# Attention and feed-forward on one core: half chunk joined, table silu in four units, later rows turned by transfers, the triangle zeroed by GpSimd

## The chip, the cores and the metric

The kernel runs on one core of a Trainium2 chip. The core has TensorE (PE: matmul, with its own weight-load row PEld), VectorE (DVE), ScalarE (ACT), GpSimd (POOL), the queue of SyncE (SP), which here issues all transfers, and 16 DMA engines. The metric is the device time of one launch in microseconds (us), lower is better. The three timed runs of the kernel before gave 602.13 (median), 602.00 and 602.32 us.

## The reference

Four sequences (b) of 512 tokens with 256 features go through six residual sublayers:

```python
x = x + 0.5 * L0_ffn(layernorm(x))       # silu(gate) * up, int weights with per-row scales, 704 hidden
x = x + L0_attn(layernorm(x))            # 16 heads of 16, rope, causal softmax
x = x + 0.5 * L0_ffn(layernorm(x))
x = x + 0.5 * L1_ffn(layernorm(x))       # sigmoid(x1) * x2, ternary weights, 704 hidden
x = x + L1_attn(layernorm(x))            # 16 query heads on 4 key heads, alibi, causal softmax, bias
x = x + 0.5 * L1_ffn(layernorm(x))
```

All values are float32 in the reference. The kernel multiplies in float16 with each activation split into a high part and the rest (a low part), so most products are made twice.

## The kernel before

Each of the four sequences is one tile of 512 tokens as four blocks of 128 (`X[:, 4*b + t, :]`). There are 16 feed-forward units (`FFNS`, counted f) and 8 attention units (`ATT`, counted n, four of layer 0 and then four of layer 1). Nothing loops: each engine has a string in `ORDER` in which one letter is one step, and runs its steps strictly in that order. Steps of different engines meet through counting semaphores. Independent sequences are interleaved, so that TensorE always has a step of some unit. `banks` gives each TensorE step its bank of PSUM (8 banks of 128x512 float32).

A feed-forward unit: DVE statistics (`N`), POOL scale and offset (`r`, four small operations), ACT normalizes into `XN` (`X`, four activations), PE turns `XN` with eight 128x128 transposes against the identity (`t`, L498), ACT writes the high part `XT` (`x`, L703), DVE the low part (`t`, L871). The 704 hidden rows are five chunks of 128 and one of 64. PE makes gate (`g`) and up (`G`) of a chunk with four matmuls of 512 columns each (L520); for the chunk of 64 rows each of `g` and `G` is eight matmuls of 64x256, the two halves of the tokens put into the two halves of the output partitions (L517). ACT takes tanh of half the gate (`t`, L719 for layer 0, L721 for layer 1). In layer 0, DVE makes silu from it in a step of its own (`s`, L885) and multiplies with up (`h`, L895); in layer 1 one DVE step does it (L898). ACT writes the high part `HH[0]` (`h`, L728), POOL the low part `HH[1]` (`h`, L1018). The buffer `TH` for these has three slots. The down product is `z` (eight matmuls for the half chunk, L537) and four `d` of ten matmuls (L549).

An attention unit: `e`/`Y`/`u`/`y` do the same normalizing and turning (L1012, L696, L498, L709, L876), `q` and `v` project (L565, L581), layer 0 is rotated by rope (`p`, `q` on DVE, `s`, `a` on POOL, through the buffers `QF` and `QS`), and SP's transfers `k` stack heads into `SQ` and `SK`. Each unit then has four groups Q of four heads. For a group PE makes the scores with queries as rows in five steps (`m`, L599) for the row maxima (`MX`, DVE L940 and L944), turns the maxima (`x`), SP inserts them as one more row of `SQ` (`r`, a transfer), and PE makes the scores again with keys as rows, maximum already subtracted, in five steps (`s`, L621). Every `m` and every `s` step ends with four mask matmuls (L470) that add -1e30 above the diagonal. ACT takes the exponential of two banks at a time into `PB` (`e`, L764, 128x1024), and PE multiplies with V (`p`, L639), which waits for the group's five exponentials only. ACT copies the result (`o`, L774). The softmax denominators go through SP (`D`, `S`, `R`: `DC`, a scratch in HBM, and back broadcast as `RB`), POOL divides (`c`, L1050) and splits (`C`, L1054), PE projects (`o`, L654) and DVE adds to `X` (L957).

## Time and profile of the kernel before

| | us |
|---|---|
| median of three timed runs | 602.13 |
| the profiled execution, its own time | 603.93 |
| its span in the trace | 601.9 |
| PE busy | 552.0 |
| DVE busy | 448.0 |
| ACT busy | 393.6 |
| POOL busy | 285.8 |

The trace shows the profiled execution. Busy time of PE is modelled with the tail of each pipelined matmul, so a row of consecutive matmuls costs less than its count times its mean; the start of the next group says what it cost. Each wait in the trace names what released it.

### The profile page before, as it was taken

The numbers are of one execution on the slowest core, as the hardware profiler recorded it, in microseconds if no ns is written. First come the engines' busy times: TensorE is split into PE (matmuls) and PEld (weight loads), VectorE is DVE, ScalarE is ACT, GpSimd is POOL, SyncE is SP. The second block draws the span as 40 slices with busy tenths as digits, with TensorE's granted clock in tenths as the row PEclk, the third lists the DMA queues.
The fourth block names the chain that finished last, engine by engine and source line by source line (L and its number), as shares of the span: only waits on it lengthen the run. The fifth ranks groups of instructions, "written<-read, shape, count | busy, mean of one in ns | idle before, by whom it ended". The sixth has DMA issues, their size and how long they took to land.

```text
span 601.9 us, 14116 instructions
## 1 busy us (share of the span) xinstructions
PE 552.0 (92%) x5772; PEld 317.3 (53%) x5772; DVE 448.0 (74%) x778; ACT 393.6 (65%) x628; POOL 285.8 (47%) x311
## 2 busy tenths in 40 slices
PE   2898888988899999999999999999999999899996
PEld 1455444455554756465654564656555556554554
DVE  4799998986788749985798786876777787773343
ACT  5776443674587666867487758478577676779442
POOL 5596989532477275842613345352333331025433
PEclk9999989998999999999999999999999999999999
DMA  8600010020121000211011011000200112010100
GB/s 337 282 2 2 35 71 25 31 79 15 38 75 71 21 19 2 89 60 43 1 67 41 30 32 53 23 17 29 78 21 20 38 67 75 21 41 18 73 36 35
DMA packets 17183, 31.82 MB, mean 53 GB/s; under 512 B 4656, under 2 KB 6064, under 8 KB 16968
## 3 DMA queue, kind: packets, MB, share of 16 engines
q1 hardware_dynamic: 17120, 30.93, 13.9%
q8 instruction: 45, 0.74, 0.5%
q14 instruction: 18, 0.15, 0.1%
HBM read 13.75 MB, written 2.36 MB: 27 GB/s over the span
## 4 chain that ended last, share of the span: by engine, by line
PE 46%; DMA 14%; DVE 12%; ACT 10%; POOL 8%; issue 6%; SPq 2%; POOLq 0%; DVEq 0%; ACTq 0%
PE PS L520 14%; PE PS L639 8%; DMA RB<-scratch 7%; PE PS L549 7%; ACT PB L764 5%; DMA scratch<-DC 3%; PE PS L565 3%; DVE MX L944 3%; PE PS L599 3%; PE PS L621 3%; PE PS L654 3%; DMA DC<-OT 2%; POOL OC L1050 2%; PE PS L470 2%; DVE XT L871 2%
## 5 line engine op out<-in xcount | busy, mean ns | idle before, releaser
L764 ACT ACTIVATE PB<-PS 128x1024 f32<-128x1024 f32 x160 | 156.4, 1028 | 42.0 <-PE PS L470 41.4
L944 DVE TENSOR_REDUCE MX<-PS 128x2 f32<-128x1024 f32 (+2 forms) x192 | 157.1, 863 | 19.5 <-PE PS L470 18.9
L520 PE MATMUL PS<-XT,WGU 128*128 128x512 f16 x640 | 151.1, 384 | 3.9 <-ACT TH L721 1.3
L1018 POOL TENSOR_TENSOR HH<-TH,HH 128x512 f16<-128x512 f32 (+1 forms) x96 | 104.2, 1101 | 85.7 <-ACT HH L728 85.6
L520 PEld LDWEIGHTS PS<-XT,WGU 128*128 128x128 f16 x640 | 58.8, 99 | 73.9 <-issue 4.6
L470 PE MATMUL PS<-MASKM,MASKW 64*128 64x128 bf16 (+1 forms) x1280 | 82.1, 206 | 0.0
L728 ACT ACTIVATE HH<-TH 128x512 f16<-128x512 f32 (+1 forms) x96 | 56.2, 595 | 32.6 <-PE PS L549 14.0
L549 PE MATMUL PS<-WD,HH 128*128 128x256 f16 x640 | 76.0, 274 | 1.0 <-POOL HH L1018 1.0
L639 PE MATMUL PS<-PB,V 128*32 128x512 f32 (+3 forms) x1024 | 75.5, 436 | 0.7 <-ACT PB L764 0.5
L470 PEld LDWEIGHTS PS<-MASKM,MASKW 64*128 64x128 bf16 x1280 | 57.7, 95 | 25.6 <-issue 0.8
L549 PEld LDWEIGHTS PS<-WD,HH 128*128 128x128 f16 x640 | 60.9, 98 | 11.8 <-POOL HH L1018 1.5
L599 PE MATMUL PS<-SK,SQ 63*128 63x256 f16 (+3 forms) x512 | 59.9, 302 | 6.8 <-DVE MX L944 2.9
L621 PE MATMUL PS<-SQ,SK 64*128 64x384 f16 (+3 forms) x512 | 58.8, 303 | 7.0 <-ACT PB L764 2.9
L898 DVE SCALAR_TENSOR_TENSOR TH<-TH,PS 128x512 f32<-128x512 f32 (+1 forms) x48 | 30.4, 642 | 42.5 <-PE PS L520 20.5
L1050 POOL TENSOR_TENSOR OC<-OC,RB 128x512 f32<-128x512 f32 x16 | 20.3, 1272 | 78.6 <-DMA RB<-scratch 78.6
L639 PEld LDWEIGHTS PS<-PB,V 128*32 128x32 f32 x1024 | 30.1, 110 | 41.8 <-issue 32.0
L565 PE MATMUL PS<-XT,WA 128*128 128x512 f16 (+1 forms) x168 | 42.7, 397 | 2.8 <-ACT OT L774 1.4
L498 PE MATMUL PS<-ID,XN 128*128 128x128 f32 x192 | 29.3, 288 | 14.5 <-ACT XN L689 11.2
L940 DVE TENSOR_REDUCE MX<-PS 128x4 f32<-128x1024 f32 x32 | 38.9, 1216 | 2.9 <-PE PS L470 2.9
L689 ACT ACTIVATE XN<-X,OFF,YR 128x256 f32<-128x256 f32 x64 | 33.1, 593 | 11.7 <-POOL OFF L1000 11.7
L788 DVE BATCH_NORM_STATS2 ST<-X 128x6 f32<-128x256 f32 x96 | 33.7, 412 | 6.7 <-DMA X<-x_in 5.9
L719 ACT ACTIVATE TH<-PS,SGH 128x512 f32<-128x512 f32 (+1 forms) x48 | 30.3, 648 | 10.3 <-POOL HH L1018 8.2
(99 smaller groups left out, 726.4 us busy)
## 6 DMA issues: line engine op xcount, KB each, us to landing
SQ<-QPB SPq DMA_DIRECT2D x24, 256.0 KB, 2.4
OC<-OT SPq DMA_DIRECT2D x16, 256.0 KB, 2.4
RB<-scratch SPq DMA_DIRECT2D x32, 128.0 KB
SK<-QPB SPq DMA_DIRECT2D x12, 256.0 KB, 2.3
out<-X SPq DMA_DIRECT2D x4, 512.0 KB, 3.3
PB<-wd SPq DMA_DIRECT2D x2, 768.0 KB, 8.9
PB<-gu SPq DMA_DIRECT2D x2, 704.0 KB, 5.9
X<-x_in SPq DMA_DIRECT2D x2, 512.0 KB, 5.2
```

What stands on the lines that cost most here:

```text
L470: m = e.matmul(to, MASKW[64 * z:64 * z + 64, way, half, :], by, start=False, stop=True, skip_group_check=True)
L520: m = e.matmul(o[:, :], WGU[l][:, k, col:col + P], XT[0][j][:, k, :], start=first, stop=last)
L549: m = e.matmul(o[:, z, q * D:(q + 1) * D], HH[j][:, s * T + t * P:s * T + (t + 1) * P], WD[l][:, s, :], start=False, stop=s == FC - 2 and ...
L565: m = e.matmul(o[0:width, :], WA[l][:, jw, k, ch * P:ch * P + width], XT[1][jx][:, k, :], start=s == 0 and k == 0, stop=s == 2 and k == 1)
L599: e.matmul(o[:, z, col:col + kw], SQ[n % 2][64 * z:64 * z + QROWS - 1, 2 * g + pr, t * P:(t + 1) * P], SK[n % 2][64 * z:64 * z + QROWS - 1 ...
L621: e.matmul(o[:, z, col:col + T - kb * P], SK[n % 2][64 * z:64 * z + QROWS, 2 * g + pr if l == 0 else pr, kb * P:(kb + 1) * P], SQ[n % 2][6 ...
L639: m = e.matmul(o[32 * a:32 * a + 32, kb * P:T], V[:, kb, 4 * g + a if l == 0 else a, :], PB[i % 2][:, s, a % 2, col:col + T - kb * P], sta ...
L728: e.activation(HH[0][:, s * T:s * T + wd], TH[:, i % 3, 0:wd], ACT.Copy).then_inc(f_hi, 1)
L764: e.activation(PB[Q % 2][:, j, :, :], two_banks("s", i), ACT.Exp, scale=0.25).then_inc(a_exp, 1)
L940: e.tensor_reduce(MX[:, Q % 4, :, :, 1], o.rearrange("p a (r k) -> p a r k", r=2), AX.X, ALU.max, negate=True).then_inc(a_max, 1)
L944: e.tensor_reduce(MX[:, Q % 4, :, pr, t], o[:, :, col:col + (t + 1) * P], AX.X, ALU.max, negate=True).then_inc(a_max, 1)
L1018: e.tensor_tensor(HH[1][:, s * T:s * T + wd], TH[:, i % 3, 0:wd], HH[0][:, s * T:s * T + wd], ALU.subtract).then_inc(f_lo, 1)
```

## The change

Five things change, and all order strings and bank numbers are written anew.

1. Half chunk joined. The weight columns are laid out so that the 64 gate columns and the 64 up columns of the half chunk lie side by side. One `g` of four 512-column matmuls makes both (gate in partitions 0 to 63, up in 64 to 127); `G` exists for five chunks only. ACT and DVE now work on 64x512 for this chunk where they worked on 128x256. Its low part is made by DVE (`k`, a new step) and not by POOL, into partitions 64 to 127 of `HH[0]`, so that one matmul per token block does high and low of it in the down product: `z` is gone and `d` has eleven matmuls. `d` takes one bank for two token blocks.
2. Table silu. In the first four units (`SILU = 4`) ACT applies Silu itself, and the DVE step `s` is dropped there. Exponentials wait until the last of these has run.
3. Rows turned by transfers. From feed-forward unit 6 on (`TF`) and for the four layer-1 attention units (`TA`), ACT writes the high half of `XN` and DVE the low half as float16 into buffers that lie over `QF` and `QS`, 128x1024 each, and SP issues one transposing transfer for each half (`T`, `U`). PE's transposes of these units are dropped.
4. Exponentials above the diagonal zeroed on POOL. The mask matmuls after `s` are dropped, except in group 0 of each layer-1 unit. In the 28 other groups POOL's new step `f` sets the upper triangle of each diagonal block of `PB` to zero, and `p` waits for it.
5. Orders and banks anew.

```diff
+SILU = 4
+TF, TA = 6, NB
+CUTS = [(1, [(0, T, 4), (2 * T + 384, T, 2)]), (3, [(4 * T, T, 4), (6 * T + 384, T, 2)]), (4, [(8 * T, 256, 4)])]
+CUTQ = [Q for Q in range(4 * NA) if ATT[Q // 4][1] == 0 or Q % 4 > 0]
 # orders: the first line of PE, before and after
-        "ttGgggggGGGgGGagzttGGgggddddGgggGGGzttggddddguuagGGqqvvGggGGqGztqtuugggGqqGdGddmdGmgmmmmxgqmmssmsmsqx"
+        "ttgGggGGGaggGgttGGddggGddggagGgGtutuddddqvgggGqGGvggqGgGqttuuddddGqqgggggmmGgqmGGmGmmqxmmmssmsmxmssm"
 # SP
+                elif c == "T":
+                    k, j = divmod(i, 2)
+                    f = TF + k
+                    w.wait_ge(f_gate, FC * f)
+                    w.wait_ge(f_up, (FC - 1) * f)
+                    w.wait_ge(f_half[j], k + 1)
+                    e.dma_start_transpose(XT[0][j][:, :, :, :].rearrange("p t k q -> p (t k) q"),
+                                          XHF[j].rearrange("p t d -> p (t d)")).then_inc(f_dma[j], 16)
...
 # PE, gate and up
-                            if s == FC - 1:
-                                for z in range(2):
-                                    m = e.matmul(o[64 * z:64 * z + 64, 0:256], WGU[l][:, k, col:col + 64],
-                                                 XT[0][j][:, k, 256 * z:256 * z + 256], start=first, stop=last)
-                            else:
-                                m = e.matmul(o[:, :], WGU[l][:, k, col:col + P], XT[0][j][:, k, :],
-                                             start=first, stop=last)
+                            m = e.matmul(o[:, :], WGU[l][:, k, col:col + P], XT[0][j][:, :, k, :],
+                                         start=j == 0 and k == 0, stop=j == 1 and k == 1)
...
 # PE, scores with keys as rows
-                    m = mask(o, 1, [col for pr, kb, col in SSTEP[j]])
+                    if l == 1 and g == 0:
+                        m = mask(o, 1, [col for pr, kb, col in SSTEP[j]])
 # PE, product with V
+                    w.wait_ge(a_tri, NTRI * sum(Q <= i for Q in CUTQ))
 # ACT
+                    if f < SILU:
+                        e.activation(TH[0:rows, i % 3, :], src, ACT.Silu, scale=SG1[0:rows, s:s + 1]).then_inc(f_tanh, 1)
+                    e.activation(XHF[0], XN[0][:, :, :], ACT.Copy).then_inc(f_half[0], 1)
 # DVE
+                    e.tensor_tensor(XHF[1], XN[0][:, :, :], XHF[0], ALU.subtract).then_inc(f_half[1], 1)
+                    e.tensor_tensor(HH[0][64:P, (FC - 1) * T:FC * T], TH[0:64, FC * i % 3, :], hi,
+                                    ALU.subtract).then_inc(f_lh, 1)
 # POOL
+                elif c == "f":
+                    j, Q = i % NTRI, CUTQ[i // NTRI]
+                    st, cuts = CUTS[j]
+                    w.wait_ge(a_exp, NS_T * Q + st + 1)
+                    for c0, d, nb in cuts:
+                        blk = PB[Q % 2][:, :, :, :].rearrange("p s z (b n) -> p (s z b) n", n=P)[:, c0 // P:c0 // P + (nb - 1) * d // P + 1:d // P, :]
+                        m = e.affine_select(blk, blk, [[0, nb], [1, P]], ALU.is_ge, 0.0, base=0, channel_multiplier=-1)
+                    m.then_inc(a_tri, 1)
```

Three places show how the orders moved. TensorE in the middle of the attention work, before: every score step is followed by its masks (L621 with L470 behind it).

```order
L621 MATMUL PS<-SQ,SK 128x512 x2
L470 MATMUL PS<-MASKM,MASKW 128x64 x4
L621 MATMUL PS<-SQ,SK 128x384 x2
L621 MATMUL PS<-SQ,SK 128x128 x2
L470 MATMUL PS<-MASKM,MASKW 128x2x64 x4
L565 MATMUL PS<-XT,WA 128x512 x6
```

And after, where `s` is L674, `m` is L652 and the masks are L538:

```order
L674 MATMUL PS<-SQ,SK 128x384 x2
L674 MATMUL PS<-SQ,SK 128x128 x2
L674 MATMUL PS<-SQ,SK 128x512 x2
L674 MATMUL PS<-SQ,SK 128x384 x2
L674 MATMUL PS<-SQ,SK 128x128 x2
L694 MATMUL PS<-PB,V 32x512 x4
L694 MATMUL PS<-PB,V 32x384 x4
L694 MATMUL PS<-PB,V 32x256 x4
L694 MATMUL PS<-PB,V 32x128 x4
```

Score steps of the second kind now follow each other with nothing between them; the masks stay behind the first kind.

GpSimd around a middle attention unit, before (L1018 low part of the hidden values, L991 to L1000 and L1006 to L1012 scale and offset, L1030 to L1038 rope, L1050 and L1054 the attention output):

```order
L1018 TENSOR_TENSOR HH<-TH,HH 128x256
L1034 TENSOR_TENSOR QF<-QF,QS 128x512
L1018 TENSOR_TENSOR HH<-TH,HH 128x512
L1054 TENSOR_TENSOR CH<-OC,CH 128x512
L1038 TENSOR_TENSOR QPB<-QF,QPB 128x512
L1018 TENSOR_TENSOR HH<-TH,HH 128x512 x4
L991 TENSOR_SCALAR VE<-MV 128x4
```

And after (L1149 the selects, L1121 the low part, L1110 to L1116 scale and offset, L1162 the division):

```order
L1149 AFFINE_SELECT PB<-PB 128x4x128
L1121 TENSOR_TENSOR HH<-TH,HH 128x512 x3
L1149 AFFINE_SELECT PB<-PB 128x4x128
L1149 AFFINE_SELECT PB<-PB 128x2x128
L1162 TENSOR_TENSOR OC<-OC,RB 128x512
L1149 AFFINE_SELECT PB<-PB 128x4x128
L1149 AFFINE_SELECT PB<-PB 128x2x128
L1110 TENSOR_SCALAR VE<-MV 128x4
L1111 TENSOR_SCALAR OFF<-MV 128x4
L1113 TENSOR_TENSOR YR<-VE,HALF 128x4
L1116 TENSOR_TENSOR OFF<-OFF,YR 128x4
L1149 AFFINE_SELECT PB<-PB 128x4x128
```

The selects stand between the division, the scale and offset of the next unit and the low parts, five to a group.

SyncE's queue in layer 1, before (L424 the maxima row, L431 and L435 out of `OT`, L441 and L450 to and from the scratch):

```order
L431 DMA DC<-OT 64x1x64
L435 DMA OC<-OT 128x1x512
L424 DMA SQ<-NM 2x8x128
L441 DMA scratch<-DC 64x64
L450 DMA RB<-scratch 64x1x512 x2
L424 DMA SQ<-NM 2x8x128 x2
```

And after (L499, L503, L474, L509, L518 for the same, L483 and L492 the new transfers for feed-forward and attention):

```order
L483 DMA_TRANSPOSE XT<-QF 128x8x128 x2
L499 DMA DC<-OT 64x1x64
L503 DMA OC<-OT 128x1x512
L474 DMA SQ<-NM 2x8x128
L509 DMA scratch<-DC 64x64
L483 DMA_TRANSPOSE XT<-QF 128x8x128 x2
L474 DMA SQ<-NM 2x8x128
L518 DMA RB<-scratch 64x1x512 x2
```

The transposing transfers stand ahead of the denominators' way out, and between its way out and its way back.

## Rows read from the trace of the kernel before

**Rows 1.** The page, part 1: busy time, share of span, instructions.
```profile
PE 552.0 (92%) x5772; PEld 317.3 (53%) x5772; DVE 448.0 (74%) x778; ACT 393.6 (65%) x628; POOL 285.8 (47%) x311
```

**Rows 2.** Windows of five stretches: length, then busy us (instructions) of each engine, clock, DMA.
```profile
15.00:92.00 77.00, 68.75 (x430) 38.39 (x429) 71.30 (x135) 46.77 (x83) 59.37 (x59) 0.98 0.19 77
...
110.00:330.00 220.00, 208.31 (x2360) 120.66 (x2355) 174.16 (x302) 151.30 (x237) 107.99 (x115) 0.99 0.12 43
330.00:550.00 220.00, 212.71 (x2500) 122.26 (x2494) 160.78 (x263) 155.78 (x246) 75.11 (x85) 1.00 0.11 39
550.00:602.00 52.00, 45.03 (x349) 27.32 (x348) 19.23 (x35) 23.48 (x42) 21.16 (x22) 0.99 0.11 42
```

**Rows 3.** The page, part 4: the chain that ended last, by engine.
```profile
PE 46%; DMA 14%; DVE 12%; ACT 10%; POOL 8%; issue 6%; SPq 2%; POOLq 0%; DVEq 0%; ACTq 0%
```

**Rows 4.** Timeline of PE at 373 us: start, us, group.
```profile
373.36 0.61 PE L537 MATMUL PS<-WD,HH 64*128 64x256 f16 x8
373.81 0.38 PE L621 MATMUL PS<-SQ,SK 64*128 64x256 f16 x4
374.03 0.28 PE L470 MATMUL PS<-MASKM,MASKW 64*128 64x128 bf16 x4
374.14 0.38 PE L599 MATMUL PS<-SK,SQ 63*128 63x512 f16 x2
374.36 0.22 PE L470 MATMUL PS<-MASKM,MASKW 64*128 64x64 bf16 x4
374.42 0.38 PE L599 MATMUL PS<-SK,SQ 63*128 63x384 f16 x4
...
376.52 4.54 PE L549 MATMUL PS<-WD,HH 128*128 128x256 f16 x40
380.90 1.04 PE L498 MATMUL PS<-ID,XN 128*128 128x128 f32 x8
381.87 0.64 PE L639 MATMUL PS<-PB,V 128*32 128x512 f32 x4
```

**Rows 5.** Timeline at 33 us, PE's rows of the half chunk.
```profile
33.70 0.63 PE L517 MATMUL PS<-XT,WGU 128*64 128x256 f16 x8
...
34.26 1.90 PE L520 MATMUL PS<-XT,WGU 128*128 128x512 f16 x8
...
36.00 4.53 PE L549 MATMUL PS<-WD,HH 128*128 128x256 f16 x40
```

**Rows 6.** Groups by shape: busy us, mean ns of one, idle before and its releaser.
```profile
L885 DVE SCALAR_TENSOR_TENSOR TH<-TH,PS 128x512 f32<-128x512 f32 x40 | 26.7, 681 | 6.0 <-ACT TH L719 5.8
L898 DVE SCALAR_TENSOR_TENSOR TH<-TH,PS 128x256 f32<-128x256 f32 x8 | 3.3, 416 | 4.3 <-PE PS L517 1.9 <-ACT TH L721 1.3 <-PE PS L520 1.1
L764 ACT ACTIVATE PB<-PS 128x1024 f32<-128x1024 f32 x160 | 156.4, 1028 | 42.0 <-PE PS L470 41.4
L790 DVE TENSOR_REDUCE FM<-X 128x64 f32<-128x1024 f32 x8 | 9.6, 1202 | 0.0
L1018 POOL TENSOR_TENSOR HH<-TH,HH 128x512 f16<-128x512 f32 x80 | 93.6, 1187 | 47.6 <-ACT HH L728 47.5
L1018 POOL TENSOR_TENSOR HH<-TH,HH 128x256 f16<-128x256 f32 x16 | 10.7, 671 | 38.1 <-ACT HH L728 38.1
L974 POOL MEMSET SK<- 128x1024 f32 x4 | 3.7, 952 | 0.0
L667 ACT ACT_TABLE_LOAD x1 | 1.3, 1283 | 0.7 <-PEq L1179 0.7
```

**Rows 7.** The page, part 6: the stacking transfers: count, size, us to landing.
```profile
SQ<-QPB SPq DMA_DIRECT2D x24, 256.0 KB, 2.4
```

**Rows 8.** Timeline of the tail, all engines.
```profile
574.03 4.54 PE L549 MATMUL PS<-WD,HH 128*128 128x256 f16 x40
577.85 2.07 ACT L689 ACTIVATE XN<-X,OFF,YR 128x256 f32<-128x256 f32 x4 [4.83 <-POOL OFF L1000]
582.99 8.81 PE L520 MATMUL PS<-XT,WGU 128*128 128x512 f16 x40
```

293 lines of the change are left out of this document (181 added, 112 removed).

## The prediction

> **What bounds the kernel now.** I read the page's busy times first [rows 1]. The reader sees TensorE at 552.0 of 601.9 us, so its idle time is 49.9 us; the next engine, DVE, has 448.0. Then the stretches [rows 2]. In the attention work from 110 to 550 us PE is busy 208.3 + 212.7 = 421.0 of 440 us, 96%, while DVE has 335.0, ACT 307.1 and POOL 183.1. There only less PE work or dearer waiting moves the time. From 15 to 92 us (the first feed-forward units and the preparation of the weights) the picture is another one: DVE is busy 71.3 of 77 us, PE 68.8. The chain that ended last gives PE 46%, DMA 14%, DVE 12%, ACT 10%, POOL 8% [rows 3]: 8% and 14% are what the path already spends on the two resources that this change loads. Last, the timelines for what a group of matmuls really costs, from its start to the next group's start, since a single one's mean holds the tail of the pipeline.
>
> **Masks after `s`.** A two-block mask starts at 374.03 and the next group at 374.14: 0.11 us. A one-block mask is 374.36 to 374.42: 0.06 us [rows 4]. A group of heads has three of the first and two of the second, 0.45 us. Dropped in 28 of 32 groups: 12.6 us of PE.
>
> **Transposes.** Eight take from 380.90 to 381.87, 0.97 us [rows 4]. Ten feed-forward and four attention units lose theirs: 14 x 0.97 = 13.6 us of PE.
>
> **Half chunk.** Eight matmuls of L517 start at 33.70, the next group at 34.26: 0.56 us, some of it the switch to the wide form [rows 5]. The two steps `g` and `G` cost 1.12. Eight wide matmuls take 34.26 to 36.00, so 0.2175 each [rows 5], and the joined step costs 0.87. Saved: 0.25 x 16 = 4.0 us. It is no more because the two 64-column halves already run side by side (eight of 256 columns in 0.56 us). In the down product `z` took 373.36 to 373.81, 0.45 us, and the four matmuls that replace it cost 4 x 4.38 / 40 = 0.44 (from 376.52 to 380.90) [rows 4]: nothing. PE together: 12.6 + 13.6 + 4.0 = 30.2 us, leaving 521.8.
>
> **DVE.** Table silu drops 24 steps, 20 of 681 ns and 4 of about 416: 15.3 us, all before the attention work [rows 6]. The half chunk widens 20 remaining DVE steps (16 products, 4 silu) from 256 to 512 columns, 681 - 416 = 265 ns each: +5.3. The new step `k` is a 512-column subtraction, taken at 681 too: 16 x 0.681 = +10.9. The low halves of the turned rows were 28 steps of the same width (19.1 us) and become 14 of 1024 columns, for which the nearest rows give 1.20 (one input) and 2 x 0.681 = 1.36 us: +16.8 to +19.1. I take the latter, the same kind of operation. DVE ends up 0.9 us higher over all, but 15.3 - 6 x (0.265 + 0.681) = 9.6 us lower in the first stretch. There PE, with 8.3 us idle and six units' half chunks less (1.5 us), becomes the bound quickly. I take 5 us for the shortened idle, between 0 (the waits are then on POOL or the weights) and 8.3.
>
> **ACT.** Fourteen 1024-column activations at 1.03 (the exponential's row) replace 28 of half the width; 32 half-chunk steps widen, at DVE's 265 ns about 8.5 us. ACT has 307 of 440 us in the attention work and absorbs it. The change of function adds two table loads of 1.28 us [rows 6], 2.6 us. The order puts the first before the first Silu and the second before the first exponential. Both can lie in a wait for PE; I charge 1.3, bounds 0 and 2.6.
> The Trainium skill's page "ScalarE: Activation LUTs" (What ACT_TABLE_LOAD costs) gives 1,283 ns for the load, as the row does, and about 1,380 ns of drain with it. By it two switches would cost 5.3 us, 2.7 more than by the row; no row here shows the drain.
>
> **POOL.** It loses 16 low parts of 671 ns, 10.7 us. It gains 28 groups x (three selects of 512 columns and two of 256). The trace has no select. Below stands the memset, 952 ns for 1024 columns, hence 0.48 and 0.24: 1.9 us a group, 53 us. Above stand the two-input subtractions of 1187 and 671 ns [rows 6]: 4.9 us a group, 137 us. A select reads once and writes once, between the two; I take the middle, 3.4 us a group, 95 us. POOL comes to 285.8 - 10.7 + 95 = 370, not the bound. But it works in order: a select that waits for its exponential holds up the low parts behind it (`HH`, hence the `TH` slot and the down product), and the division of the attention output. And `p` now waits for the last select, 0.5 to 1.2 us after the last exponential.
>
> **Transfers.** 28 new ones of 256 KB. A stacking transfer of that size lands after 2.4 us [rows 7]. Before, the last row of `XT` was ready 582.99 - 579.92 = 3.1 us after `XN` was finished [rows 8]. Now: 1.03 for the high half, about 1.3 for the low, 2.4 for its landing: 4.7, so 1.6 us later. In 13 of 14 places other units' work covers this on PE. In the tail PE was idle from 578.57 to 582.99 except for the transposes. The new order leaves 20 wide matmuls (4.4 us) beside the 44 of the down product (4.8) for this stretch, 9.2 us instead of 4.8, so the tail is covered as well: 0, and 3 us if that cover fails.
> The Trainium skill's page "Advanced Engine Details and Errata" (X-Bar Transpose) says that transposing transfers run as fast as regular ones, but its section on software and hardware descriptor generation calls the hardware queue the worse one for transposes. The first agrees with my use of the stacking row; the second, which has no figure, speaks against this change. No row here shows either.
>
> **What the attention work gives back.** PE's demand there falls from 421 by 12.6, by 12.6 of the transposes (one tail unit apart) and by about 2.5 of the half chunks, to 393 us. The others stay: DVE 335 + 6, POOL 183 - 7 + 95 = 271. At today's 96% that would take 411 us; DVE would then be at 83%, where it was 76%. With less slack on DVE and the select in every group's path I expect PE at 93.5%: 420 us, 9 to 10 us given back. Bounds: 0, and the whole 28.
>
> **The sum**, on the span: 601.9 - 30.2 - 5.0 + 1.3 + 10.0 = 578.0. The timed median stands 0.2 us above the span, and so I forecast 578.
>
> **Rivals.**
> A, everything is gained: selects near the memset's price, and the attention work stays at 96%. Then 578 - 10 - 3 = 565. For it: PE's waits now are short and spread. Against: one more engine in every group.
> B, POOL takes PE's place in the path: selects at the subtraction's price. POOL in the attention work is then 183 - 7 + 137 = 313 of 412 us, the `p` steps wait 0.4 to 0.8 us in each of 28 groups and the low parts behind them: 12 us more given back, 590. For it: POOL's 8% of the chain. Against: POOL was idle for 257 of 440 us.
> C, slower: a transposing transfer holds the SP queue. The 28 stand in that queue ahead of the maxima row and of the denominators' way out and back, which the chain already holds with 14%. With a hold of h us each, all on the path, the 24 us of gain are gone at h = 0.86; at 2 us it is 578 + 56 - 24 of slack that the maxima row has = 610. For it: nothing in the trace shows how such a transfer is issued. Against: a plain one of this size has landed after 2.4 us [rows 7], so its own hold is shorter, and most of the 28 would have to stand on the path.
> That the change doesn't do what it says: the instructions are plainly gone from PE, so this has no share of its own.
>
> **Chances.** Forecast (568 to 586) 0.55; A 0.12; B (586 to 601) 0.13; C above 603.3 0.15; and 0.05 for an end within 0.2% of 602.13, which is about what a measurement of this kernel can tell from no change. Faster by more: 0.80. The range leaves out C (0.15) and the lower third of A (0.05): 562 to 602.
>
> **What would show each step.** PE's busy time near 522 and 560 fewer masks; first exponential about 5 us earlier and DVE under 90% in the first stretch; a select of 512 columns between 0.5 and 1.2 us, and `p` released by POOL for under 0.5 us in the mean; transposing transfers landing near 2.4 us with SP never blocked by them; PE above 93% of the attention work. What would make me wrong: selects above 1.2 us, transfers above 4 us, or new orders whose waits have nothing to do with these five steps.

## The result, and the profile after

The changed kernel takes 611.58 us (median of 4 runs, 610.09 to 612.43), the kernel before beside it 602.07. The ratio is 1.0156, 95% interval 1.0135 to 1.0177: slower by 9.5 us, where the forecast was 578 and the range ended at 602. The profiled execution's span is 610.0 us against 601.9.

First the page after, its busy times (they answer to [rows 1]), TensorE's granted clock in 40 slices, and the chain that ended last ([rows 3]):

```profile
PE 531.2 (87%) x4844; PEld 285.7 (47%) x4844; DVE 456.0 (75%) x758; ACT 401.0 (66%) x616; POOL 354.2 (58%) x435
PEclk9988999799979999999999999799999999999999
PE 33%; DVE 16%; POOL 15%; ACT 15%; DMA 10%; issue 9%; SPq 2%; POOLq 0%; DVEq 0%; ACTq 0%
```

PE has lost 20.8 us of busy time where my sum took 30.2 away, and its idle time rose from 49.9 to 610.0 - 531.2 = 78.8 us. The mean granted clock fell from 0.991 to 0.972: in six stretches, 34.0 us together, PE ran at 1.2 instead of 2.4 GHz, and it was busy for 29.0 us of them. PE's share of the chain fell from 46% to 33%, and POOL's rose from 8% to 15%.

The same three stretches as in [rows 2], after (length, busy us of PE, PEld, DVE, ACT, POOL, clock, DMA share, GB/s):

```profile
15.00:92.00 77.00, 66.11 (x375) 38.93 (x373) 61.00 (x116) 47.67 (x83) 60.77 (x61) 0.93 0.20 78
110.00:330.00 220.00, 198.08 (x1956) 106.14 (x1953) 172.30 (x276) 152.08 (x227) 137.23 (x178) 0.96 0.19 54
330.00:550.00 220.00, 202.11 (x2095) 106.17 (x2091) 175.42 (x275) 157.55 (x239) 109.76 (x141) 0.98 0.23 56
```

DVE in the first stretch is where I expected it (71.30 - 9.6 = 61.7, here 61.00), and PE there has not become faster. In the attention work PE is busy 91% of the time, where I took 93.5%.

The groups that are new after, with the mean ns of one, how long `p` waits for a select (idle us, times; the matmuls' row PE and the weight loads' row PEld, whose waits can lie side by side), and the transposing transfers with their us to landing:

```profile
L1149 POOL TENSOR_SCALAR_AFFINE_SELECT PB<-PB 128x512 f32<-128x512 f32 x84 | 55.6, 662 | 58.9 <-ACT PB L841 58.7
L1149 POOL TENSOR_SCALAR_AFFINE_SELECT PB<-PB 128x256 f32<-128x256 f32 x56 | 22.8, 407 | 0.0
L1001 DVE TENSOR_TENSOR HH<-TH,HH 64x512 f16<-64x512 f32 x16 | 15.1, 942 | 1.0 <-ACT HH L804 0.6
L952 DVE TENSOR_TENSOR QF<-XN,QF 128x1024 f16<-128x1024 f32 x10 | 16.1, 1607 | 4.3 <-ACT QF L763 4.2
L957 DVE TENSOR_TENSOR QS<-XN,QS 128x1024 f16<-128x1024 f32 x4 | 4.9, 1221 | 1.6 <-ACT QS L769 1.5
...
  PE PS L694: 6.4, 6
  PEld PS L694: 2.9, 2
...
XT<-QF SPq DMA_TRANSPOSE x20, 3.2
XT<-QS SPq DMA_TRANSPOSE x8, 3.3
```

To see where the time went, three marks are read from each trace: the start of the first `p`, the start of the last group's `p`, and the span's end. Kernels built for the experiments are in the table too; the ratio is to the kernel before, timed beside each.

| kernel | ratio, 95% interval | first `p` at | from there to the last group's `p` | from there to the end |
|---|---|---|---|---|
| before | 1 | 114.8 | 438.6 | 48.5 |
| after | 1.0156 (1.0135 to 1.0177) | 122.4 | 434.0 | 53.6 |
| a_nosel | 1.0019 (0.9984 to 1.0054) | 120.5 | 426.0 | 53.0 |
| a_masks | 1.0025 (0.9998 to 1.0053) | 120.2 | 426.0 | 53.5 |
| a_selfew | 1.0011 (0.9976 to 1.0046) | 121.8 | 428.0 | 52.1 |
| a_seltiny | 1.0060 (1.0016 to 1.0104) | 121.7 | 425.5 | 53.7 |
| a_selmove | 1.0133 (1.0083 to 1.0182) | 121.5 | 433.1 | 53.2 |
| a_plain | 1.0147 (1.0096 to 1.0198) | 121.8 | 436.0 | 53.4 |
| a_silu0 | 1.0424 (1.0372 to 1.0476) | 137.9 | 436.0 | 53.7 |
| m_tail | 1.0015 (0.9980 to 1.0051) | 121.5 | 428.3 | 54.2 |
| m_noturn | 1.0281 (1.0216 to 1.0345) | 120.7 | 439.0 | 57.3 |
| b_nomask | 0.9869 (0.9826 to 0.9913) | 112.4 | 430.7 | 48.0 |
| b_sel | 1.0256 (1.0186 to 1.0326) | 113.4 | 454.4 | 49.5 |
| b_selfew | 0.9999 (0.9966 to 1.0033) | 115.1 | 438.0 | 48.4 |
| b_silu | 1.0058 (1.0033 to 1.0083) | 114.5 | 442.1 | 47.9 |
| b_turn | 1.0281 (1.0218 to 1.0343) | 114.4 | 455.5 | 47.8 |
| o_hs | 1.0127 (1.0052 to 1.0202) | 118.6 | 441.0 | 47.5 |
| b_banks | 1.0152 (1.0079 to 1.0226) | 118.9 | 440.1 | 47.9 |

Marks come from one execution each; those of kernels that are the same up to a mark differ by up to 2.7 us there (112.4 to 115.1), so smaller differences say nothing. For a_seltiny and a_masks the traced execution was also the fastest of ten.

The changed kernel loses 7.6 us before the first `p`, gains only 4.6 in the attention work where 28 us of PE's work are gone, and loses 5.1 at the end. Split in the same way, my sum had -5.2 (-5.0, -1.5 and +1.3), -17.7 (-27.7 and +10) and -1.0. So it misses by 13 us at the start, 13 in the attention work and 6 at the end.

### The profile page after: what moved, and what is told of

It is laid out like the page before. It is cut to its first block, busy times and chain, and to the rows that moved or that the text cites. A ratio compares the mean times of both kernels' runs of the same rounds, so it can differ in the third digit from the quotient of the medians.

```text
span 610.0 us, 12425 instructions
## 1 busy us (share of the span) xinstructions
PE 531.2 (87%) x4844; PEld 285.7 (47%) x4844; DVE 456.0 (75%) x758; ACT 401.0 (66%) x616; POOL 354.2 (58%) x435
## 4 chain that ended last, share of the span: by engine, by line
PE 33%; DVE 16%; POOL 15%; ACT 15%; DMA 10%; issue 9%; SPq 2%; POOLq 0%; DVEq 0%; ACTq 0%
PE PS L582 10%; PE PS L694 7%; PE PS L602 6%; ACT PB L841 5%; DVE MX L1048 5%; DMA RB<-scratch 4%; POOL PB L1149 3%; PE PS L674 2%; POOL HH L1121 2%; PE PS L652 2%; PE PS L618 2%; DMA scratch<-DC 2%; DVE TH L990 2%; POOL OC L1162 2%; POOL X L1129 2%
## 5 line engine op out<-in xcount | busy, mean ns | idle before, releaser
L582 PE MATMUL PS<-XT,WGU 128*128 128x512 f16 x704 | 167.5, 384 | 11.8 <-DVE XT L961 3.4
L1121 POOL TENSOR_TENSOR HH<-TH,HH 128x512 f16<-128x512 f32 x80 | 98.2, 1240 | 78.8 <-ACT HH L804 78.4
L1149 POOL TENSOR_SCALAR_AFFINE_SELECT PB<-PB 128x512 f32<-128x512 f32 (+1 forms) x140 | 74.8, 560 | 58.9 <-ACT PB L841 58.7
L582 PEld LDWEIGHTS PS<-XT,WGU 128*128 128x128 f16 x704 | 64.6, 99 | 92.4 <-issue 7.4
L602 PE MATMUL PS<-WD,HH 128*128 128x256 f16 x704 | 84.8, 276 | 5.3 <-POOL HH L1121 4.3
L602 PEld LDWEIGHTS PS<-WD,HH 128*128 128x128 f16 x704 | 67.7, 99 | 19.5 <-POOL HH L1121 5.7
L674 PE MATMUL PS<-SQ,SK 64*128 64x384 f16 (+3 forms) x512 | 59.5, 306 | 17.7 <-ACT PB L841 6.1
L652 PE MATMUL PS<-SK,SQ 63*128 63x256 f16 (+3 forms) x512 | 61.4, 305 | 9.7 <-ACT PB L841 3.1
L804 ACT ACTIVATE HH<-TH 128x512 f16<-128x512 f32 (+1 forms) x96 | 58.7, 624 | 12.6 <-DVE TH L996 5.7
L538 PE MATMUL PS<-MASKM,MASKW 64*128 64x128 bf16 (+1 forms) x720 | 46.6, 207 | 0.0
L1162 POOL TENSOR_TENSOR OC<-OC,RB 128x512 f32<-128x512 f32 x16 | 20.8, 1298 | 38.7 <-DMA RB<-scratch 38.7
L538 PEld LDWEIGHTS PS<-MASKM,MASKW 64*128 64x128 bf16 x720 | 32.9, 96 | 15.8 <-issue 1.5
L674 PEld LDWEIGHTS PS<-SQ,SK 64*128 64x128 f16 x512 | 18.4, 95 | 46.7 <-issue 16.9
L797 ACT ACTIVATE TH<-PS 128x512 f32<-128x512 f32 (+1 forms) x48 | 27.5, 589 | 16.7 <-PE PS L582 10.2
```

What stands on the lines that cost most here:

```text
L538: m = e.matmul(to, MASKW[64 * z:64 * z + 64, way, half, :], by, start=False, stop=True, skip_group_check=True)
L582: m = e.matmul(o[:, :], WGU[l][:, k, col:col + P], XT[0][j][:, :, k, :], start=j == 0 and k == 0, stop=j == 1 and k == 1)
L602: m = e.matmul(o[:, q * D:(q + 1) * D], HH[j][:, s * T + t * P:s * T + (t + 1) * P], WD[l][:, s, :], start=ci == 0, stop=ci == FC - 1 and ...
L652: e.matmul(o[:, z, col:col + kw], SQ[n % 2][64 * z:64 * z + QROWS - 1, 2 * g + pr, t * P:(t + 1) * P], SK[n % 2][64 * z:64 * z + QROWS - 1 ...
L674: m = e.matmul(o[:, z, col:col + T - kb * P], SK[n % 2][64 * z:64 * z + QROWS, 2 * g + pr if l == 0 else pr, kb * P:(kb + 1) * P], SQ[n % ...
L804: e.activation(HH[0][0:rows, s * T:(s + 1) * T], TH[0:rows, i % 3, :], ACT.Copy).then_inc(f_hi, 1)
```

## Experiments: the selects

**Leaving them out, and undoing the part.** Both kernels drop every `f` from GpSimd's order and take `CUTQ` empty; a_masks has TensorE's masks again:

```diff
-CUTQ = [Q for Q in range(4 * NA) if ATT[Q // 4][1] == 0 or Q % 4 > 0]
+CUTQ = []
-                    if l == 1 and g == 0:
+                    if Q not in CUTQ:            # a_masks only
                         m = mask(o, 1, [col for pr, kb, col in SSTEP[j]])
```

> The changed kernel without its 84 selects: GpSimd leaves them out and TensorE's `p` waits for none of them, everything else and every other place in the orders as it is. What is left out: nothing above the diagonal is hidden in the 28 groups, so their sums are wrong. Theory O (the new order leaves TensorE in clustered gaps, whatever the parts cost): the two longest gaps in front of `p` that a select ends (1.6 and 2.6 us in the changed kernel's trace) go, little else, 605 to 611 us against 611.6. Rival S (the selects on GpSimd are what cost the time): nearly the whole 9.5 us over the kernel before go, and more with the masks gone: 602 us or less.

> The changed kernel with one part undone: the second pass of all 32 groups is masked by TensorE again, as before, and the 84 selects are gone; everything else and the places in the orders as they are. Theory O: 12.6 us of mask matmuls come back to TensorE (0.45 us for each of 28 groups, worked out from the trace of before) and some of them fall into gaps that were idle: 613 to 622 us. Rival S: the selects cost more than the masks they replaced, so the time falls below 610 us.

Measured: 603.83 and 603.18 us. Theory O is wrong here and rival S right in the main: nearly the whole loss over the kernel before goes with the selects, 7.8 us, though leaving the masks out as well brings nothing more. With the masks back on PE, 12.6 us of work by my sum, the time is the same as without any. From 110 to 550 us PE of a_masks:

```profile
110.00:330.00 220.00, 205.73 (x2356) 116.93 (x2358) 177.82 (x289) 155.25 (x232) 99.18 (x103) 0.99 0.20 56
330.00:550.00 220.00, 205.25 (x2304) 112.11 (x2301) 169.38 (x262) 160.44 (x243) 77.40 (x83) 1.00 0.24 57
```

It is 411.0 of 440 us busy, with 29 us free: in this order the masks fall into free time.

**The same in the order before.** b_nomask leaves the masks of the same 28 groups out of the kernel before; b_sel puts the selects into GpSimd's order there too, each where its exponential had ended; b_selfew has them in 15 groups and masks in the rest.

```diff
 # b_nomask
+                    if l == 1 and g == 0:
                         m = mask(o, 1, [col for pr, kb, col in SSTEP[j]])
 # b_sel, b_selfew besides
+                    w.wait_ge(a_tri, NTRI * sum(Q <= i for Q in CUTQ))   # ahead of p
+CUTQ = [0, 2, 3, 7, 8, 9, 10, 11, 12, 13, 15, 17, 19, 21, 30]           # b_selfew
 ... (POOL's step f, and f put into its order)
```

> The kernel before with the second pass's masks left out in the same 28 of 32 groups and nothing put in their place (no selects); orders, banks and all else as they are. What is left out: nothing above the diagonal is hidden in those groups. If TensorE bounds the attention stretch as my prediction's sum took it (the term of 12.6 us for the masks, 0.45 us for each group), the time falls by about that: 588 to 592 us. Theory F (TensorE has free time there that the masks fall into, as putting them back into the changed kernel cost nothing, 603.2 against 603.8 us): 599 to 602 us.

> The kernel before with the change's fourth part alone: the 28 groups' masks of the second pass taken from TensorE and the 84 selects put into GpSimd's order of before, each at the place where its exponential had ended; banks and all other orders as they are. With the masks simply left out this order gained 7.8 us. Theory S2 (from the last exponential over the last select to `p` take 0.85 us in place of 0.05, and in 15 of 28 groups of the kernel before `p` came sooner than 0.85 us after it): some 8 us are given back, 600 to 606 us. Rival S1 (only the new order's queue made the selects dear): 594 to 599 us.

> The kernel before with selects in 15 groups alone, those in whose group `p` started 0.85 us or more after the last exponential in the trace of before (groups 0, 2, 3, 7 to 13, 15, 17, 19, 21, 30), and TensorE's masks in the other 17. By S2 the selects then cost nothing and 15 of 28 groups' masks are saved: 15/28 of the 7.8 us, 4 us, 597 to 600 us, faster than with all 28. By S1 it saves about half of what the kernel with all selects saves, and is slower than that one.

Measured: 595.66, 618.59 and 603.41 us. So in the old order the masks are worth 1.3%, 7.9 us (5.3 to 10.5), not 12.6 and not 0. The selects give back 23 us there (1.0256 - 0.9869 = 3.9%), three times what S2 said. b_selfew equals the kernel before: its 15 selects cost no more than their masks did, but the 4 us I expected did not come. In five of the 15 groups `p` still starts within 0.15 us of the select's end, since POOL came to it late (group 11: 1.94 us after the exponential's end).

What PE and PEld wait for in b_sel ahead of `p` (first and last start; idle us, times; 12.6 us in 14 places are the row PE's own), and one place, POOL and then PE (start, us, group, idle before):

```profile
L645 PE MATMUL PS<-PB,V x1024: 272/486/1061, 113.4 to 569.9; 128*32 128x512 f32 x43, 128*32 128x256 f32 x43, 128*32 128x128 f32 x43, 128*32 128x384 f32 x42
...
  POOL PB L1052: 13.7, 16
...
468.55 2.35 POOL L1060 TENSOR_TENSOR X<-X,BO 128x1024 f32<-128x1024 f32 x1 [2.29 <-ACT XN L702]
470.86 1.58 POOL L1052 TENSOR_SCALAR_AFFINE_SELECT PB<-PB 128x512 f32<-128x512 f32 x3
...
472.58 2.99 PE L645 MATMUL PS<-PB,V 128*32 128x512 f32 x17 [2.31 <-POOL PB L1052]
```

The last exponential of that group ended at 468.37 + 1.91 = 470.28. The bias addition had started at 468.55 and held POOL to 470.86, and then the selects took their turn. In 18 of 28 groups of b_sel `p` starts within 0.15 us of the last select's end, so the select holds it.

**Which selects cost in the changed kernel.** The same reading of the trace after: in ten groups `p` starts 0.15 us or less after the last select (8 to 12, 19, 23, 26, 30, 31; in group 23 PE waits 0.06 us, and it is left aside). The longest wait, group 19, POOL and then PE:

```profile
379.74 1.27 POOL L1162 TENSOR_TENSOR OC<-OC,RB 128x512 f32<-128x512 f32 x1 [2.99 <-DMA RB<-scratch]
381.09 0.19 POOL L1095 TENSOR_SCALAR VE<-MV 128x4 f32<-128x4 f32 x1
381.37 0.23 POOL L1099 TENSOR_SCALAR OFF<-MV 128x4 f32<-128x4 f32 x1
381.57 1.04 POOL L1101 TENSOR_TENSOR YR<-VE,HALF 128x4 f32<-128x4 f32 x1
...
382.89 1.58 POOL L1149 TENSOR_SCALAR_AFFINE_SELECT PB<-PB 128x512 f32<-128x512 f32 x3
...
385.48 1.08 PE L694 MATMUL PS<-PB,V 128*32 128x512 f32 x4 [2.63 <-POOL PB L1149]
```

The group's first exponentials had ended at 377.3. POOL stood 3.0 us waiting for the denominators' transfer (`c`), then did the normalization's four small operations, and then five selects in a row. In a_nosel the same `p` follows its neighbour at once:

```profile
374.85 0.22 PE L536 MATMUL PS<-MASKM,MASKW 64*128 64x64 bf16 x4
375.00 1.39 PE L692 MATMUL PS<-PB,V 128*32 128x512 f32 x12
```

From the last exponential's end to `p` it is 0.64 us there and 3.35 in the changed kernel. Over the nine groups such differences come to 7.0 us, 6.0 of them in the four (8, 11, 12, 19) whose selects stood behind other POOL work.

Three kernels ask whether the place in the queue, the step's length or its load does it. a_selfew masks the nine groups on TensorE and drops their selects alone; a_selmove moves selects ahead at three places of GpSimd's order; a_seltiny keeps all waits and narrows each select to 4 columns:

```diff
 # a_selfew
+CUTQ = [0, 1, 2, 3, 4, 5, 6, 7, 13, 14, 15, 17, 18, 21, 22, 23, 25, 27, 29]
 # a_selmove, GpSimd's order in groups 8, 11, 19
-...fhfhCdcdffsC...    ...hhhfcfefhhb...    ...ffdfdcrfffr...
+...fhfhCdfcdfsC...    ...hhhffcfehhb...    ...ffdfdfcrffr...
 # a_seltiny
-                        m = e.affine_select(blk, blk, [[0, nb], [1, P]], ALU.is_ge, 0.0, base=0, channel_multiplier=-1)
+                        m = e.affine_select(blk, blk, [[0, nb], [1, 4]], ALU.is_ge, 0.0, base=0, channel_multiplier=0)
```

> The changed kernel with nine of its 28 groups masked on TensorE again (groups 8 to 12, 19, 26, 30, 31): those in whose group `p` started 0.15 us after the end of the last select, or 0.06 us in the one of the 2.6 us wait, so that the select alone held it; the other 19 groups keep their selects, all else and all orders as they are. Theory S2 (a select costs where it is the last thing that `p` waits for, and nowhere else): the whole 7.8 us that the selects cost come back, 602.5 to 605 us. Rival S3 (the selects' load on GpSimd costs too): two thirds of the load stays, so 606 us or more.

> The changed kernel with GpSimd's order changed at three places: in the groups 8, 11 and 19 the selects go ahead of two `c`, one `d`, one `e` and one `r` step, where their exponentials had ended before those steps began. Theory S1 (the selects cost time where they stand in GpSimd's queue behind other work, and TensorE's `p` waited 0.7, 1.6 and 2.6 us for them there): 4 to 6 us come back with the lowered clock behind those waits, 605 to 608 us. Rival S2 (the step from the last exponential over a select to `p` costs in every group, wherever the selects stand): within 2 us of 611.6. Rival S3 (what GpSimd does in the selects' 75 us delays its other steps): also near 611.6.

> The changed kernel with every select narrowed from 128 to 4 columns of each block, so that its wait for the exponential, its place in the order and `p`'s wait for it stay and most of GpSimd's time for it goes. What is changed in the computation: the exponentials above the diagonal are hardly zeroed. Theory S1 (the queue ahead of the selects): the c, e and r steps ahead stay, so most of the loss stays, 607 to 611 us. Rivals S2 in its duration (0.66 us of the last select on the way to `p`) and S3 (75 us of GpSimd time): near the 603.8 us of the kernel without selects, 602 to 606 us.

Measured: 603.81, 610.66 and 606.34 us. a_selfew is the decisive one: 57 of the 84 select steps stay, a load of two thirds, and the loss is gone. So the loss belongs to the nine groups whose `p` waits for a select; the GpSimd time of the other 19 costs nothing that can be measured. That the selects of the nine also held up other GpSimd steps is not ruled out by this run alone.

Moving them ahead brought 1 us in place of 4 to 6, less than two such runs can tell apart. In group 11 the wait changed its name. a_selmove, POOL, then ACT, then PE:

```profile
262.47 0.99 POOL L1148 TENSOR_SCALAR_AFFINE_SELECT PB<-PB 128x512 f32<-128x512 f32 x2 [3.10 <-ACT PB L840]
263.43 1.70 POOL L1161 TENSOR_TENSOR OC<-OC,RB 128x512 f32<-128x512 f32 x1
...
265.16 0.63 ACT L855 ACTIVATE CH<-OC 128x512 f16<-128x512 f32 x1 [2.76 <-POOL OC L1161]
265.69 1.00 ACT L840 ACTIVATE PB<-PS 128x1024 f32<-128x1024 f32 x1
...
266.75 0.39 PE L651 MATMUL PS<-SK,SQ 63*128 63x384 f16 x4 [1.68 <-ACT PB L840]
```

The division `c` came later, ACT's high half `CH` waited for it, the next exponential stood behind `CH` in ACT's queue, and PE waited 1.68 us for that one. In group 19 my move was incomplete (two of three steps still stood behind the normalization), and 2.23 of 2.63 us stayed. a_seltiny keeps 1.6 us of PE's waits, in groups 11 and 19, where the changed kernel has 6.4. Of the ratio's 1.4% over a_nosel 1.0% goes (1.0060 against 1.0156), so the selects' own length has the clear share. What is left for the queue ahead of it, 0.4%, is within the intervals; there only the two waits in the trace speak for it.

## Experiments: the turned rows

a_plain issues the 28 transfers as plain ones of the same bytes; m_tail gives the last feed-forward unit's turn back to PE in a_masks; m_noturn gives all 14 back; b_turn makes 8 turns by transfers in the old order, where the rows were ready 10 us ahead.

```diff
 # a_plain
-                    e.dma_start_transpose(XT[0][j][:, :, :, :].rearrange("p t k q -> p (t k) q"),
-                                          XHF[j].rearrange("p t d -> p (t d)"))
+                    e.dma_start(XT[0][j][:, :, :, :].rearrange("p t k q -> p (t k q)"),
+                                XHF[j].rearrange("p t d -> p (t d)"))
 ... (the same for U; ACT scales by 2^-8 and DVE multiplies in place of subtracting)
 # m_noturn, besides a_masks' edits; orders and banks too
-TF, TA = 6, NB
+TF, TA = 16, 8
 # b_turn; orders and the steps T and U besides
+TF, TA = [8, 10, 11, 12, 13], [5, 6, 7]
```

> The changed kernel with the 28 transposing transfers of `T` and `U` issued as plain transfers of the same 256 KB between the same tiles. What is changed in the computation: the rows come unturned, and the low half is a product with rows scaled down by 2^8 in place of a difference, so the output is wrong; the same instructions otherwise. Theory O: SP no longer holds 1.2 to 2.0 us for each of them and the landing goes from 3.2 to about 2.4 us, which was hidden mostly: 608 to 612 us. Rival C (transposing transfers hold SP's queue and load the DMA engines, which was my third rival): 5 us or more come back, 606.5 us or less.

> The kernel with the changed kernel's orders and the masks back on TensorE (603.2 us), with the rows of the last feed-forward unit turned by TensorE again in place of two transposing transfers; nothing else moved. In the trace the way from that unit's last normalised row to its first activation took 6.4 us over transfers and took 3.2 us in the kernel before over TensorE. Theory O (in the tail nothing covers the transfers): 2 to 4 us less, 599 to 601.5 us. Rival (the transfers are hidden there too, the tail is set by GpSimd's low halves): 602.5 to 604 us.

> The kernel with the changed kernel's orders and the masks back on TensorE (603.2 us), with the turns of all ten later feed-forward units and four later attention units given back to TensorE, ScalarE and VectorE, placed where the transfers were issued, and the banks assigned anew. If the turns are worth on the path what my sum gave (14 times 0.97 us, 13.6 us), the time rises to 613 to 620 us. Rival (TensorE has free time there, as for the masks in this order): 600 to 607 us.

> The kernel before with the turns of five later feed-forward units (8, 10 to 13) and three attention units (5 to 7) done by transposing transfers, where the trace of before leaves 10 us or more from the last normalised row to the unit's first activation; each half's cast and transfer stand where the rows are ready, banks and orders otherwise as they are. TensorE is spared 8 times 0.97 us. In the new order the transfers were worth 16 us for 14 units. Theory T (they gain wherever the rows are ready early): 594 to 599 us, which would beat both kernels. Rival C (SP's queue is held 1.3 us by each and attention's own transfers stand behind them, and the halves' one long step holds ScalarE and VectorE): 602 to 608 us.

Measured: 610.44, 604.26, 619.51 and 619.87 us. a_plain's transfers land sooner and the time does not change, so in the new order the transposing form costs nothing that can be measured (the two intervals leave room for some 4 us). The trace after does show small waits of PE for the turned rows, 2.7 us in 4 places, which a_plain has not:

```profile
XT<-QF SPq DMA_DIRECT2D x20, 256.0 KB, 2.4
```

m_tail is a miss, and its rows say why. PE, then ACT's first activation of the unit:

```profile
576.83 1.70 PE L578 MATMUL PS<-ID,XN 128*128 128x128 f32 x8
578.32 4.82 PE L614 MATMUL PS<-WD,HH 128*128 128x256 f16 x33
582.98 9.66 PE L594 MATMUL PS<-XT,WGU 128*128 128x512 f16 x44
...
584.04 0.59 ACT L810 ACTIVATE TH<-PS 64x512 f32<-64x512 f32 x1 [4.88 <-PE PS L594]
```

The rows are turned by 579.9, and the unit's first `g` still stands behind the previous unit's down product until 582.98. That product was what covered the transfers. m_noturn says that in the new order the 14 turns are worth 2.6% (1.0281 - 1.0025), 13.0 us of it in the attention work (439.0 against 426.0). Its banks were assigned anew, which can be up to 1.5% by the control below but is 1.5 us in the attention work. So my 13.6 us agree with it, but the total alone would allow anything from about 6 us up.

b_turn says the opposite for the old order: 17 us lost, all in the attention work, more than even its rival expected. SP's queue there, in the kernel before and then in b_turn, and what PE waited for:

```profile
497.68 0.56 SPq L435 DMA_DIRECT2D OC<-OT  x1
498.29 0.60 SPq L424 DMA_DIRECT2D SQ<-NM  x1
```

```profile
508.65 0.57 SPq L479 DMA_DIRECT2D OC<-OT  x1
509.33 1.33 SPq L459 DMA_TRANSPOSE XT<-QF  x1
510.71 0.60 SPq L450 DMA_DIRECT2D SQ<-NM  x1
511.36 1.24 SPq L459 DMA_TRANSPOSE XT<-QF  x1
...
512.54 0.39 PE L665 MATMUL PS<-SQ,SK 64*128 64x512 f16 x2 [1.35 <-DMA SQ<-NM]
...
517.84 10.43 SPq L450 DMA_DIRECT2D SQ<-NM  x2
...
523.87 0.39 PE L665 MATMUL PS<-SQ,SK 64*128 64x512 f16 x2 [3.35 <-DMA SQ<-NM]
```

The maxima row `SQ<-NM` stands behind a transfer that holds the queue 1.3 us, PE waits 1.35 us for the row, and the next row, issued 0.1 us behind a 512 KB transfer of the output (517.29 to 517.75), is 3.35 us late. The first of these is my third rival, in an order that has no room for it; in the changed kernel's it does not show in the time. In all, PE waits 7.5 us in 3 places for a maxima row there, against 1.9 us in one place before; the rest of the 17 us I haven't followed. The changed kernel has 4.3 us of such waits in 3 places and a_plain 3.1 in one.

## Experiments: the silu, the half chunk, the banks

a_silu0 takes the silu out of the changed kernel; b_silu puts it alone into the kernel before (three units); o_hs is that with the half chunk joined too; b_banks is the kernel before with new banks only. For b_silu:

```diff
+SILU = 3
+                    if f < SILU:
+                        w.wait_ge(p_sc, 1)
+                        e.activation(TH[:, i % 3, 0:wd], src, ACT.Silu, scale=SG1[:, s:s + 1]).then_inc(f_tanh, 1)
```

> The changed kernel with the table silu undone: the four first feed-forward units take tanh and VectorE's `s` step again (24 steps of about 0.7 us each on VectorE, two table loads fewer on ScalarE), `s` standing in VectorE's order where ScalarE had the silu ready. Theory O: VectorE was busy 61.0 of the 77 us of the first stretch and gets 16 us more to do, so it sets that stretch: 615 to 626 us. Rival T (the silu gains nothing where it stands, since VectorE has idle time): within 2 us of 611.6.

> The kernel before with the table silu alone, in the three first units: VectorE's 18 `s` steps there go (11.4 us of its time), ScalarE loads one more table on each side of the silus, orders otherwise and banks as they are. With the half chunk joined as well the old order took 1.3 per cent more than before. If VectorE's saved time shortens the way to the first `p` (my 5 us), 596 to 600 us. Rival (TensorE and ScalarE hold the first stretch in this order, and the table loads of 1.3 us stand on the way): 601 to 604 us, and the loss of the two parts together is then the half chunk's.

> The two first parts alone, in the orders of the kernel before: half chunk joined and table silu in the three first units (the fourth's silu would need the order of the exponentials changed), masks and PE turns as before. VectorE's new `k` step stands where its input is ready, GpSimd's short `h` and TensorE's `z` are dropped, and the banks are assigned anew, since the joined `g` keeps a bank longer. My sum has 4.0 us for the half chunk on TensorE and 5 us of idle time less before attention: 593 to 598 us. Theory O says the order must be remade for the parts: TensorE waits more where `g`, `h` and `k` come late, 603 to 612 us.

> A control: the kernel before with its banks assigned anew by the rule that assigned those of the two kernels that needed new ones (half chunk with silu in the old order; turns given back to TensorE), 535 of 698 entries different, and nothing else. If the assignment is neutral, 601 to 605 us, and the 1.3 and 2.8 per cent of those two kernels are their parts' own. If it costs the 4 us that a model of the waits gives it, 605 to 609 us, and about that much is to be taken off both.

Measured: 627.84, 606.38, 610.08 and 610.48 us. The changed kernel's order needs the silu: without it the first `p` comes 15.5 us later. But the silu alone brings nothing in the old order. The first stretch of b_silu, beside that of [rows 2]:

```profile
15.00:92.00 77.00, 69.03 (x433) 38.59 (x434) 63.63 (x118) 47.63 (x84) 59.83 (x60) 0.98 0.20 78
```

DVE is busy 7.7 us less than the 71.30 of before, PE as much as before (69.03 and 68.75), and the first `p` starts at 114.5 against 114.8. So DVE's busy time did not set that stretch; the two table loads that came in, 2.6 us, can't have hidden 7.7. Over all b_silu is 0.6% slower; where, I can't say, its difference lies behind the first `p`.

o_hs was expected to tell the half chunk's price, and the control takes that away: b_banks has only other bank numbers and is as slow, with the same marks (118.9, 440.1, 47.9 against 118.6, 441.0, 47.5). Its numbers come from the same rule as those of o_hs but are not the same ones. If both cost alike, half chunk and silu together are worth nothing, within 1% (their two intervals together); else the half chunk's price is not known. The banks alone cost 1.5% (0.8 to 2.3%), 4 us of it before the first `p`.

## Experiments: orders made by a model

A small model of the waits, with durations from these traces, gave the kernel before 603 us and the one after 609. I let it rearrange orders and banks for a_masks (s_masks) and for the changed kernel (s_sel) by many small moves.

```diff
 ORDER = {
-    ...the changed kernel's strings...
+    ...rearranged strings and banks...
```

> The same code as the kernel that had the changed kernel's orders and the masks back on TensorE (603.2 us: joined half chunk, table silu in four units, later rows turned by transfers, masks on TensorE), with all five engines' orders and the banks rearranged over many small steps by a model of the waits whose durations come from the traces of this case. The model takes 8 us off. Theory O (the parts save TensorE's time and the given order leaves it idle): 592 to 599 us, with TensorE's idle time down by as much. Rival (the parts themselves are worth nothing, idle time only changes place): 602 us or more.

> The changed kernel's code with all its parts, the selects among them, and with the orders and the banks rearranged in the same manner; the model takes 11 us off. If the selects cost only where they stand in the order (theory S1), this kernel falls below the one without them, 590 to 600 us. If they cost in every group, because the last of them stands between the last exponential and `p` (0.64 us and 0.15 us after it), it stays above that kernel, 600 to 606 us.

Measured: 613.45 us (1.0193, 1.0122 to 1.0264) and 617.17 us (1.0245, 1.0186 to 1.0305). Both are slower than where they started: the 8 and 11 us that the model promised did not come. Whether the model's errors did it or the new bank numbers, which cost 1.5% in b_banks, is not separated. Their first `p` comes at 126.9 and 131.4 against 120.2 and 122.4. That s_sel stays above s_masks fits S2, but these two runs settle nothing. No kernel here beats the one before and does the whole work.

## Why the prediction was wrong

The sum was 601.9 - 30.2 - 5.0 + 1.3 + 10.0 = 578.0. Step by step:

- **PE's work, -30.2.** The instructions went as counted, 560 masks among them. I had PE at 521.8 busy; it is 531.2, and 525.8 in a_nosel, which has the same PE instructions at a mean clock of 0.986 where the changed kernel has 0.972. I had no term for the clock. It fell behind two of the long waits for selects (at 271.9 us behind group 11's, at 384.6 in group 19's), where a_nosel has no such stretch, so a waiting PE pays twice there. But three of the six stretches at 1.2 GHz lie ahead of the first `p`. The median clock of all executions is 0.991 to 0.994 for the kernel before, 0.980 for a_masks, 0.974 for a_nosel and 0.969 after, so most of its fall comes with the new order and not with the selects.
- **The selects: the failed step that the runs show best.** I priced POOL's time (3.4 us a group, measured 2.8: 3 x 0.662 + 2 x 0.407) and found it covered. Outside the nine groups it is, as a_selfew shows. What I wrote down and never priced was the sentence that `p` waits for the last select; it had only an unnamed share in the 10 us of the give-back. A select costs 0.85 us on that way (0.07 for its start, 0.64, 0.15 to `p`) where an exponential costs 0.05, and more when POOL is in the middle of something else: 1.3 to 1.4% in the new order, 8 us on top of a give-back that was above 10 already, and 3.9% in the old one. With the masks worth nothing (below), the part that I had at -12.6 plus a share of 10 came out at +8. My rival B had this mechanism at the right place, with 0.4 to 0.8 us in 28 groups; it was nine groups with up to 2.7.
- **The masks, -12.6.** In the old order they are worth 7.9 us, in the new one nothing that can be measured (a_nosel and a_masks). PE's share of 96% made me count each us of PE work nearly in full.
- **The transposes, -13.6.** Right in the new order within what m_noturn can tell. That they can lose in an order not made for them (b_turn, +17) I had as rival C, for the wrong kernel. The landing of 3.2 us in place of 2.4 and SP's hold of 1.3 us, which I had not priced, cost nothing measurable there (a_plain). The whole difference in landing is SP's longer hold: from the end of the issue to the landing it is 1.90 us for a transposing transfer into `XT` from `QF` and 1.87 for the plain one of a_plain. The Trainium skill's page "Advanced Engine Details and Errata" (X-Bar Transpose) has transposing transfers as fast as regular ones. For what follows the issue these rows agree; the section gives no price for the issue, where the difference lies.
- **The first stretch, -5.0.** It came out at +7.6, as large a miss as the attention work's. I took DVE's busy 71.3 of 77 us as what holds PE; in the old order b_silu takes 7.7 us off and nothing moves. In the new order PE has four long waits there, here in the changed kernel:

```profile
30.97 3.59 PE L582 MATMUL PS<-XT,WGU 128*128 128x512 f16 x8 [3.35 <-DVE XT L961]
46.23 3.63 PE L582 MATMUL PS<-XT,WGU 128*128 128x512 f16 x16 [1.47 <-DVE GS L914]
52.77 0.73 PE L566 MATMUL PS<-ID,XN 128*128 128x128 f32 x2 [2.47 <-ACT XN L755]
62.82 1.47 PE L618 MATMUL PS<-XT,WA 128*128 128x512 f16 x6 [1.35 <-DVE XT L966]
```

They are 8.6 us together, and 9.2 in a_masks. The last stands behind eight steps in a row with which DVE prepares layer 1's weights (a_masks, first and last of them):

```profile
49.87 0.57 DVE L939 TENSOR_SCALAR SQ<-SQ,GS 128x704 f16<-128x704 f32 x1
...
58.55 0.94 DVE L943 SCALAR_TENSOR_TENSOR WGU<-SK,GS 128x704 f16<-128x704 f32 x1
```

So the step that failed here is known, DVE's busy share read as the bound. What holds the new order back by 5.4 us in a_masks and 7.6 in the changed kernel, that placing or the banks or something else, was not tried and stays open.
- **Table loads, +1.3.** Three of 1283 ns are in the trace. No run separates them; b_silu, with two loads more, has its first `p` no later. The drain that the Trainium skill's page "ScalarE: Activation LUTs" (What ACT_TABLE_LOAD costs) adds to a load is not seen in any run here.
- **The give-back, +10.** I had PE at 93.5% of the attention work; it was 91%, at a lower clock. Of 27.7 us of work taken away there 4.6 came back as time, so 23 were given back and not 10: 8 by the selects, and 15 in a_nosel without any, about what the masks' 12.6 us make when they fall into free time.

The end: a_masks has 53.5 us after the last group's `p` against 48.5, but more of the feed-forward work stands there (unit 14's first activation comes 7.7 us after that mark, in the kernel before 3.0 us after it). From the first `p` to the end it is 7.6 us faster than the kernel before, and it loses 5.4 ahead of it.

The chances: the lower third of rival A is 0.04 and not 0.05. None of the three rivals is what came: the time was in C's range, but by B's mechanism and by a lost first stretch that had no rival, only the last sign of being wrong that I named, orders with waits of their own.

In short: without selects the new order gains in the attention work, mostly by the turned rows (m_noturn), about what it loses at the start, and the selects then add 1.3% on the way to `p`. The first part of this is a sum of marks, the second is shown by a_nosel, a_masks and a_selfew.

## What to carry to other kernels

A step put between a producer and its consumer on a third engine is not priced by that engine's load but, group by group, by the slack between the two: read from the trace how long after the producer's end the consumer starts, and leave the step out where it is under the new way's length. Here this took the loss away (a_selfew) but won nothing over the masks (b_selfew, 0.9999). A bounding engine's busy share of 96% does not mean that work taken off it comes back as time; one cheap kernel that leaves the work out (b_nomask, 7.9 of 12.6 us) tells the ceiling before anything replaces it. Keep order and banks fixed when a part is judged, and run a control when they can't be: new bank numbers alone cost 1.5% here.

## What was not expected of the hardware

- A transposing transfer of 256 KB holds SP's queue 1.23 to 1.99 us (median 1.28; a plain one of that size 0.52 in a_plain and 0.60 for the stacking) and lands 3.2 us after its issue began. The packets went from 17183 to 46745.
- A select over 512 columns takes 662 ns and over 256 columns 407, nearer to the memset's 0.48 us for 512 than to the two-input subtraction's 1187 ns.
- The mean of a group can hide two prices. `k` has a mean of 942 ns where I took 681, but nine of its 16 steps take 684 to 687 ns and six 0.98 to 1.65 us. The low halves into `QF` have a mean of 1607 ns, but seven of ten take 1.20 to 1.23 us, as those into `QS`, and three 2.0 to 3.3. Each of these nine long steps runs beside a GpSimd step with two inputs, and no step that runs alone is long, but some short ones have such a neighbour too. No run tests the cause.
- Half the partitions save nothing: 64x512 steps take as long as 128x512 ones (690 and 681 ns in a_silu0).
- The bank numbers of TensorE's outputs alone move the time by 1.5%, with PE's idle time nearly the same (b_banks: 606.9 - 555.1 = 51.8 against 49.9); the cause is open.
